# A decoder layer on one core: the last step of quantisation and the residual add move from VectorE to ScalarE and GpSimd

## The reference, cut to what matters

```python
s = sqrt(max(amax_x, EPS) / max(amax_w, EPS));  xs = x / s;  ws = w * s
x_scale = max(max(abs(xs), axis=-1), EPS) / 127          # per row, w_scale in the same way
x_q = clip(round(xs / x_scale), -127, 127)               # w_q in the same way
out = x_q @ w_q.T * x_scale * w_scale.T
```

## Time and profile before

| what | us |
|---|---|
| median of 3 runs | 1476.31 |
| lowest and highest | 1475.50, 1485.98 |
| the profiled execution | 1484.92 |
| its span, first to last instruction | 1483.2 |
| first turn | 0 to about 147 |
| merged passes | to about 308, 468 and 625 |
| ending | to about 790 |

### The profile page before, as it was taken

How to read it: one execution, slowest core, us unless ns; L and a number is a source line. 1 busy time by engine, 2 the same in 40 slices (tenths; PEclk the granted TensorE clock), 3 DMA queues, 4 the chain that set the end, 5 groups by cost and what they waited for, 6 DMA issues and landing times.

```text
span 1483.2 us, 24661 instructions
## 1 busy us (share of the span) xinstructions
PE 1339.3 (90%) x7339; PEld 992.9 (67%) x7339; DVE 888.9 (60%) x1579; ACT 411.6 (28%) x627; POOL 389.5 (26%) x478
## 2 busy tenths in 40 slices
PE   7988998999998998789978998999999999879991
PEld 3553455445454455278857887999999999768890
DVE  2542787669856887687757876334343455555634
ACT  1132133303341144212120013223222334343423
POOL 1131012200230014000001671344444344343432
PEclk9989998999989999889998999999999999999996
DMA  8431533225420632413110012645464456868437
GB/s 283 133 89 39 156 92 96 72 87 141 114 72 23 176 100 68 154 39 131 58 57 29 29 37 66 167 77 139 77 141 75 84 133 140 236 175 237 83 72 249
DMA packets 90109, 163.96 MB, mean 111 GB/s; under 512 B 8544, under 2 KB 29536, under 8 KB 89968
## 3 DMA queue, kind: packets, MB, share of 16 engines
q1 hardware_dynamic: 73168, 122.88, 26.7%
q0 software_dynamic: 16816, 39.59, 14.4%
HBM read 113.42 MB, written 49.02 MB: 110 GB/s over the span
## 4 chain that ended last, share of the span: by engine, by line
PE 68%; DVE 11%; DMA 7%; issue 7%; ACT 2%; SPq 1%; POOL 1%; DVEq 1%; ACTq 0%; POOLq 0%
PE psUA L1001 13%; PE psUB L1001 12%; PE psR L1095 11%; PE psY L1008 9%; PE psR L1008 5%; PE psR L1171 3%; PE psOT L1202 3%; PE psST L1185 3%; PE psTX L984 2%; PE psR L1109 2%; DMA kst<-scr_d 2%; PE psTH L1017 2%; DMA room<-in_L_ffn_w_dram 2%; DMA qst<-nml 1%; DVE nm L1566 1%
## 5 line engine op out<-in xcount | busy, mean ns | idle before, releaser
L1001 PE MATMUL psUA<-w_s,xgT 128*128 (+1 forms) x1284 | 244.6, 341 | 18.8 <-DVE xgT L1379 16.1
L1001 PEld LDWEIGHTS psUA<-w_s,xgT 128*128 128x128 f32 x1284 | 214.4, 196 | 27.0 <-DVE xgT L1379 15.4
L1001 PE MATMUL psUB<-w_s,xgT 128*128 (+1 forms) x1284 | 225.3, 324 | 0.0
L1001 PEld LDWEIGHTS psUB<-w_s,xgT 128*128 128x128 f32 x1284 | 211.4, 190 | 0.0
L827 POOL DMA_INDIRECT sx_d<-yg,dst_i x74 | 119.4, 1614 | 299.3 <-ACT yg L905 261.8
L867 ACT ACTIVATE silg<-psUA 128x352 f32<-128x352 f32 x107 | 49.6, 464 | 432.8 <-PE psUB L1001 432.8
L1008 PE MATMUL psY<-w_s,hgT 128*128 (+3 forms) x621 | 163.6, 408 | 0.1
L789 POOL TENSOR_SCALAR_AFFINE_SELECT pT<-pT 128x128 f32<-128x128 f32 (+1 forms) x192 | 68.5, 375 | 347.6 <-ACT pT L943 347.5
L1388 DVE SCALAR_TENSOR_TENSOR hg<-silg,cws,psUB 128x352 f32<-128x352 f32 x75 | 43.5, 579 | 174.4 <-ACT silg L867 174.4
L1566 DVE TENSOR_REDUCE nm<-psR 128x1 f32<-128x128 f32 (+3 forms) x256 | 113.1, 486 | 41.9 <-PE psR L1173 37.5
L1008 PEld LDWEIGHTS psY<-w_s,hgT 128*128 128x128 f32 (+1 forms) x621 | 114.6, 192 | 23.0 <-DVE hgT L1396 0.5
(11 more groups left out here) (218 smaller groups left out, 1901.3 us busy)
## 6 DMA issues: line engine op xcount, KB each, us to landing
room<-in_L_ffn_w_dram SPq DMA_DIRECT2D x32, 704.0 KB
scr_d<-qhl SPq DMA_DIRECT2D x32, 512.0 KB, 3.7
qst<-scr_d SPq DMA_DIRECT2D x48, 256.0 KB, 4.0
kst<-scr_d SPq DMA_DIRECT2D x48, 256.0 KB, 5.9
room<-in_L_ffn_w_dram SPq DMA_DIRECT2D x16, 512.0 KB
xt<-in_x_dram SPq DMA_DIRECT2D x5, 1024.0 KB, 7.2
xr<-in_x_dram SPq DMA_DIRECT2D x4, 1024.0 KB, 5.5
breg<-in_fside_BxS2xS_dram SPq DMA_DIRECT2D x4, 1024.0 KB, 7.1
```

The lines of the kernel that those rows point to most:

```text
L1001: mm = pe.matmul(t[:, 0:F], xgT[:, par, a_, c * P:(c + 1) * P], w[:, buf, b_, c, :], start=(c == 0 and n == 0), stop=(c == C - 1 and n == ...
```

## The change

ScalarE subtracts the rounding constant and writes bf16 (an Identity activation with the bias -12582912 from a new tile `unround`); VectorE signals it by a new semaphore after the clamp. ScalarE copies the weight scales (`wb` joins `BY_ACT`), and VectorE waits for that copy before the first `h`. GpSimd adds `x1` to `h1` by quarters, each after its `h:1:i`, and VectorE waits for the four before the statistics of ln2. The order of the steps is as before.

```diff
-        CHAIN = {"rows": 1, "ln1": 11, "ln2": 12, "s": None, "ws": ST + 2, "wq": ST + 1, "xs": 3, "xq": ST + 1,
+        CHAIN = {"rows": 1, "ln1": 11, "ln2": 11, "s": None, "ws": ST + 2, "wq": ST, "xs": 3, "xq": ST,
-        BY_ACT = {"xt", "wqt", "xqt", "x2t", "lg", "lgt"}
+        BY_ACT = {"xt", "wb", "wqt", "xqt", "x2t", "lg", "lgt"}
...
+            fill(unround[:, :], -ROUND)
...
+                    elif x[0] == "h" and x[1] == 1:
+                        i = x[2]
+                        at.let_go(pool, x)
+                        pool.tensor_tensor(h1[:, i, :], h1[:, i, :], x1[:, i, :], ALU.add).then_inc(s_res, 1)
...
+                        elif x[0] == "wb":
+                            act.copy(wsc_bc[:, :], t).then_inc(s_afree, 1)
...
+                    elif x[0] in ("wq", "xq"):
+                        n = x[1]
+                        w = I2 if n else D
+                        if x[0] == "xq":
+
+                            act.wait_ge(s_rfull, at.ticket(("wqt", n, (C2 if n else C) - 1)) + 1)
+                            apart(act)
+                        act.wait_ge(s_whole, 4 * b + 2 * n + 1 + (x[0] == "xq"))
+                        act.activation(xq[:, :, 0:w], xs[:, :, 0:w], ACT.Identity, bias=unround[:, 0:1]).then_inc(s_quant, 1)
...
-                    made(dve.tensor_scalar(v, v, -QMAX, ROUND, ALU.max, ALU.add))
-                    after()
-                    dve.tensor_scalar(q, v, -ROUND, None, ALU.add).then_inc(s_quant, 1)
+                    dve.tensor_scalar(v, v, -QMAX, ROUND, ALU.max, ALU.add).then_inc(s_whole, 1)
...
-                    elif kind == "wb":
-                        done(dve.tensor_copy(wsc_bc[:, :], t))
...
                     elif kind == "h":
+                        if c == 0:
+                            at.let_go(dve, ("wb", n))
+                            apart(dve)
...
-                        made(dve.tensor_tensor(h1[:, :, :], h1[:, :, :], x1[:, :, :], ALU.add))
-                        after()
+                        dve.wait_ge(s_res, ST * (b + 1))
+                        apart(dve)
```

More of the change, by code:

```diff
@@ L78, in decoder_layer @@
         dump = sb("dump", [P, 1])
+        unround = sb("unround", [P, 1])
         score = sb("score", [P, NT, E])
@@ L132, in decoder_layer @@
         s_quant = sem("s_quant")
+        s_whole = sem("s_whole")
+        s_res = sem("s_res")
         s_powin = sem("s_powin")
@@ L1488, in scaled, with quantised @@
                     return dve.reciprocal(rc[:, :], sc[:, :])
-                def quantised(v, q, rc):
+                def quantised(v, rc):
                     for i in range(ST):
@@ L1618, in walk @@
                         dve.wait_ge(s_dve, at.ordered(x))
-                        quantised(xs[:, :, 0:w], xq[:, :, 0:w], rws)
-                    elif kind == "wb":
-                        done(dve.tensor_copy(wsc_bc[:, :], t))
+                        quantised(xs[:, :, 0:w], rws)
                     elif kind == "xs":
@@ L1625, in walk @@
                         dve.wait_ge(s_dve, at.ordered(x))
[L1626 to L1630, removed]
+                        quantised(xs[:, :, 0:w], rxs)
                     elif kind == "h":
+                        if c == 0:
+                            at.let_go(dve, ("wb", n))
+                            apart(dve)
                         done(dve.scalar_tensor_tensor(out=h1[:, c, :], in0=t, scalar=xsc[:, c:c + 1], in1=wsc_bc[:, :],
```

## The result

The changed kernel takes 1501.18 us in the median of its runs (1497.25 to 1502.35; one disturbed run is left out here, and one of the runs beside e9 to e11), the kernel before 1475.9 beside it. The ratio is 1.0148 with an interval of 1.0088 to 1.0208. So the change costs 1.5 to 2%, 25 to 31 us. The forecast was 1485.0 with a range of 1472 to 1496, and the time lies above the range.

What follows compares the result with a forecast made beforehand. The prediction saw TensorE 90% busy and VectorE's clamp on the chain of waits, with ScalarE's fixed order delaying both. Three merged passes at +3.14, -1.0 and +0.3 in the ending gave +8.7 us on 1476.3: 1485.0, range 1472 to 1496.

Steps and rivals of the forecast that it cites:

- ScalarE's passes: Quantised values moved from VectorE: 2.04 us for 2048 columns and 1.18 us for 1024 on ScalarE.
- The low halves: VectorE's halves of qk:3, qk:5 and qk:7 wait 1.5 to 2.7 us each for ScalarE's high halves.
- wq:0: Weights, 512 columns, in a merged pass: low half 1.56 us late, row maxima 0.95 late; price +0.95 us.
- xq:0: Activations, 512 columns, in a merged pass: exponentials, xqT copies and score products delayed; price +1.25 us.
- wq:1: Weights, 256 columns, in a merged pass: wqT copy late, TensorE's product waits for it; price +0.94 us.
- ln2: Residual on GpSimd in a merged pass: statistics start where they did; price 0, between -0.3 and +0.5 us.
- Ending: Three GpSimd adds hide, winning 1.0 us; wq:0 and xq:0 ahead of the gate's SiLU cost +0.3.
- The step that failed: Last of the sum: median run taken as one without clock falls, 1476.3 + 8.7 = 1485.0 us.
- Rival (c): Clock: new TensorE gaps at 181 and 202 bring one more fall per merged pass, 5.1 us each; 1500.3; chance 0.18.
- Relief (a): VectorE sets the pace, so work taken off it pays: -6.9 us, 1469.4; chance 0.12.
- Absorbed (b): TensorE's DMA waits at scores:4 and max:12 swallow 2 of 3.14 us a pass: +2.6, 1478.9; chance 0.13.
- Ports (d): GpSimd's adds hold VectorE's evacuations of h:1, up to 3.8 us a merged pass: +11.4, 1496.4; chance 0.05.

Runs made afterwards that it cites:

- e9: Changed kernel with two useless TensorE products in the gap at 181 and one more in the gap at 206: 1.0128 of the kernel before.
- e11: Changed kernel with ScalarE issuing the high halves of qk:3, qk:5 and qk:7 ahead of its passes, run a second time: 1.0114 of the kernel before.
- e7: The changed kernel once more, unaltered, on another chip: 1.021 of the kernel before.
- e1: Kernel before with only the residual moved, GpSimd adding it by quarters: 1.0007 of the kernel before.
- e3: Changed kernel with ScalarE issuing the high halves of qk:3, qk:5 and qk:7 ahead of its passes: 1.0104 of the kernel before.
- e12: Kernel before with ScalarE copying wb:0 and making wq:0's and xq:0's values behind the high halves, GpSimd adding early residual quarters: 1.0032.
- e16: e3 with the residual back on VectorE: 1.0061 of the kernel before.
- e15: Kernel before with ScalarE copying the weight scales and GpSimd adding the first residual quarter in merged passes, three in the ending: 0.9943, 1475.5 us.
- e5: Kernel before plus a ScalarE pass that nobody reads at wq:0, xq:0 and wq:1 of each merged pass: 1.0202 of the kernel before.
- e6: Changed kernel with two useless TensorE products filling the gap at 181 in merged passes: 1.0112 of the kernel before.
- e4: Changed kernel with four useless TensorE products in the gap at 181, twice the gap's length: 1.0162 of the kernel before.

## Why the prediction was wrong, by its own steps

The prediction's own sum of waits was nearly right, and the term that it left at zero, the clock, was about twice as large.

- **ScalarE's passes**: 2.04 and 1.18 forecast, 2.00 and 1.15 measured. The low halves were to wait 1.5 to 2.7 us; they waited 2.64, 2.65 and 1.79.
- **wq:0**: +0.95 us forecast. The stage without a fall gives 13.47 - 12.59 = +0.88. **xq:0**: +1.25 forecast, +1.13, +1.08 and +1.10. **wq:1**: +0.94 forecast, +0.78, +1.39 and +1.18. The row maxima after wq:0 came 5.17 us after the clamp instead of 4.26, 0.91 later where 0.95 was forecast.
- **ln2** in a merged pass: 0 within -0.3 to +0.5 forecast, +0.20, 0.00 and +0.69 measured. The times on GpSimd were right: counted from the first evacuation of h:1, masks done after 3.0 us and the last add after 6.7 were forecast, 3.1 and 6.8 measured. What was wrong is the row it was set against. "They repeat it to 0.1 us" doesn't hold at ln2: the stage took 6.77 and 6.98 us in the two passes of the kernel before whose clock had just been low and 6.28 in the third. There the kernel before runs from 576.69 to the first row here, the kernel after from the second to the third:

```profile
582.97 2.47 DVE L1463 BATCH_NORM_STATS2 bn<-breg 128x6 f32<-128x512 f32 x4
```
```profile
589.59 0.75 DVE L1646 SCALAR_TENSOR_TENSOR breg<-psR,xsc,wsc_bc 128x512 f32<-128x512 f32 x1 [0.21 <-issue]
...
596.56 2.47 DVE L1482 BATCH_NORM_STATS2 bn<-breg 128x6 f32<-128x512 f32 x4 [3.24 <-POOL breg L789]
```

  At full clock this term is 0.7 us a pass and not 0.
- **Ending**: -1.0 + 0.3 = -0.7 forecast, 86.1 - 86.7 = -0.6 measured, and -0.9 between the last evacuation and the statistics.
- **Their sum**: 3 x 0.88 + 3.3 + 3.4 + 0.9 - 0.6 = +9.6 against +8.7 forecast, and +10.8 with 0.69 for ln2 in every pass. The two profiled executions differ by 12.3, close to that, but by luck: in this pair the falls after the new gap (5.8 us in two passes) are offset by shorter stages before h:1:0 (5.6 us), the place of the earlier trace rows, where the profile of the kernel before had its own falls.
- **The step that failed** is the last of the sum: "I take the median run to be one without these falls. Forecast for the median: 1476.3 + 8.7". It took the clock to be a matter of the one profiled execution, which the change leaves alone. But the gaps are the change's own, and the clock is the larger part of the loss: some 17 to 23 of e7's 28.2 us. Nor is a usual run of the kernel before one without falls: e1, which takes the same time, was profiled at 1477.7 us with a stage of 15.55 from wq:0 and one of 15.08 before h:1:0. On e7's chip the mean clocks of the two kernels don't overlap: 0.951 to 0.962 before, 0.940 to 0.947 after.
- **Rival (c)** named this mechanism and this place, "two new gaps of TensorE a pass, of some 1.6 us (at 181 and 202)", and gave 1500.3; measured were 1501.2. It had 0.18. Its size was right in the sum by luck, not in the parts: one more fall a pass at 5.1 us was assumed. The second gap, at 206, is 0.5 to 0.9 us in the changed kernel and not 1.6. What came was a fall of 3.0 us after 181 in 5 of 6 passes of after and e7, one of 4.7 after 206 in 1 of 6, and the rest elsewhere. The argument against it ("others (at 271) are followed by none") was one place, and it was given the weight of a rule, though two of three passes had the falls at 250.
- **Relief (a)** needs low halves without a wait; they waited. e3 shows what it would take, the high halves issued first, and that it still doesn't pay. **Absorbed (b)**: the order's price showed in full, stage by stage. **Ports (d)**: evacuations at 0.75 us beside GpSimd's adds, and e1 at 1.0007.

**What stays open.** How large each later share of the lost clock is, and whether a fall that is prevented at one place comes at another, can't be told from one profile a kernel. e3's remaining 1.1% divides into about 0.3% for xq:0 (e12) and 0.4 to 0.5% for the residual in that company (e16), both from differences of overlapping intervals; the rest has no owner. Why the clock falls after some gaps and not after others, 10 of 12 at 1.62 us and 6 of 11 at 0.89, was not settled.

## What to carry to other kernels

Before moving an operation to an idle engine, look at what stands behind it in that engine's queue: a helper with 28% load, walked in order, made the main engines wait 2.6 us for a move of 1.2. In a kernel like this one, with TensorE 90% busy, price each new gap not only by its length but by a possible fall of the granted clock after it (3 to 5 us here, after gaps of 1.6 and 0.9), and check the mean clock of many runs, not of one profile. Divide by lateness: give the helper the parts that are ready early and keep the last one on the engine that has just written it, which by the stages gave 2.6 of e15's 6.9 us.

## What the hardware showed that was not expected

- A gap of 1.6 us in a stretch where TensorE is otherwise busy is followed, in 10 of 12 passes, by 10 to 14 us at the lower clock; with useless products in the same gap no fall came in 9 of 9. e6 does more work than the changed kernel and is faster (1.0112 against 1.021 on the same chip).
- Filling the second gap too brought nothing more (1.0128): in one pass the stage before h:1 took 18.3 us instead of 11 to 16. That the fall moved there is a reading and not shown.
- A pass on ScalarE that nobody reads, three times in a merged pass, costs 2.0% of the whole kernel (e5).
- An f32 product of 512 columns shows as two matmul rows of 0.43 us each (e4, e6: eight rows in 3.6 us for four calls).
- GpSimd's three masks, which take 0.91 us elsewhere (265.93 in the kernel after), span 2.32 us beside VectorE's add of two SBUF inputs (e15, 262.07), as in the earlier trace rows; beside evacuations from PSUM its adds and theirs keep their times.
